# Four stages of a decoder kernel on one core: slot mixture, two attentions of sixteen heads of 64, and a gated attention

## The reference

```python
# L0 ffn (l0f): 64 experts x 32 slots = 2048 slots
logits = xn @ phi_w.T + phi_b            # (tokens, 2048), xn = layernorm(x)
dispatch = softmax over the 32 slots of each expert, per token
xt = dispatch^T @ xn  ->  experts  ->  val (2048, 128)
combine = softmax over the 64 experts at each slot number, per token
x += combine @ val
# L1 xattn (l1x) and L3 attn (l3a): 16 heads of 64
q, k, v = three projections of 128 -> 1024 (biases in l1x, keys of l1x from ctx)
x += softmax(causal(q k^T * scale)) v @ wf + bf
# L3 xattn (l3x): 8 heads of 16, gates from cumulative sums
D[i,j] = exp(-max(M_i - g_j, 0)) for j <= i, else 0
C = (q k^T) * D;  x += groupnorm(C v / max(|sum C|, ...))
```

## Time and profile before

| | us |
|---|---|
| median of 3 runs | 5007.74 (5003.48 to 5016.55) |
| profiled execution, its own time | 4999.0 |
| its span, first to last instruction | 4997.1 |
| window of the dispatch with its loads (574 to 936) | 362 |
| window of the combine (957 to 1410) | 453 |
| window of l1x (1661 to 2236) | 575 |
| window of l3a (3480 to 4032) | 552 |
| window of l3x, second part (4104 to 4318) | 214 |
| busy: PE 3581.9 (72%), DVE 3131.3 (63%), ACT 2404.7 (48%), POOL 2159.8 (43%) | |

### The profile page before, as it was taken

The page is one execution under the profiler, slowest core; times in us unless marked ns, Lnnn a source line. Parts: engine busy times, 40 slices in busy tenths (PEclk is TensorE's granted clock), DMA queues, the critical chain, the costliest instruction groups (busy, mean ns, idle before and its releaser), DMA issues. The chain is left out here.

```text
span 4997.1 us, 90315 instructions
## 1 busy us (share of the span) xinstructions
PE 3581.9 (72%) x28501; PEld 2648.4 (53%) x28501; DVE 3131.3 (63%) x5955; ACT 2404.7 (48%) x9569; POOL 2159.8 (43%) x2543
## 2 busy tenths in 40 slices
PE   7969677676679799971989223763999947369356
PEld 5646344465568577761656212563777723146356
DVE  6847588699957455557978622333666649878412
ACT  6959422344324477760469200221677722169235
POOL 3544288567634222221745054353232216545253
PEclk8979899888889899995989656886999969779578
DMA  6024100100000000000000510465000013120057
GB/s 82 2 38 57 31 1 1 42 1 1 1 11 2 21 4 4 4 2 3 3 13 10 92 40 29 138 191 163 1 0 0 0 43 105 44 42 2 13 196 253
DMA packets 365314, 210.42 MB, mean 42 GB/s; under 512 B 216339, under 2 KB 337452, under 8 KB 363668
## 3 DMA queue, kind: packets, MB, share of 16 engines
q1 hardware_dynamic: 351396, 180.67, 14.4%
q0 software_dynamic: 13568, 25.41, 1.5%
HBM read 156.40 MB, written 54.30 MB: 42 GB/s over the span
## 5 line engine op out<-in xcount | busy, mean ns | idle before, releaser
L2024 POOL TENSOR_TENSOR l1x_Sx<-l1x_Sx,l1x_sm 128x512 f32<-128x512 f32 x128 | 133.5, 1043 | 376.4 <-DVE l1x_sm L2167 376.4
L2024 POOL TENSOR_TENSOR l3a_Sx<-l3a_Sx,l3a_sm 128x512 f32<-128x512 f32 x128 | 133.5, 1043 | 353.5 <-DVE l3a_sm L2167 353.5
L2948 POOL DMA_INDIRECT l2f_results<-l2f_b_ys,l2f_b_xb x160 | 155.3, 971 | 217.3 <-DVE l2f_b_ys L2936 167.8
L1297 POOL TENSOR_TENSOR l0f_c_Z<-l0f_c_Z,l0f_c_shiftT 128x1024 f32<-128x1024 f32 x64 | 178.5, 2818 | 157.9 <-ACT l0f_c_shiftT L1219 157.9
L1175 PE MATMUL l0f_c_Y<-l0f_val,l0f_c_Z 128*128 128x128 f32 x1024 | 156.3, 325 | 113.7 <-DVE l0f_c_Z L1271 113.7
L1175 PEld LDWEIGHTS l0f_c_Y<-l0f_val,l0f_c_Z 128*128 128x128 f32 x1024 | 152.1, 240 | 120.2 <-DVE l0f_c_Z L1271 120.2
L2226 ACT ACTIVATE l3a_Sx<-l3a_Sx,l3a_nmx 128x128 f32<-128x128 f32 x512 | 199.2, 393 | 17.6 <-DVE l3a_nmx L2161 17.4
L2226 ACT ACTIVATE l1x_Sx<-l1x_Sx,l1x_nmx 128x128 f32<-128x128 f32 x512 | 200.1, 401 | 14.5 <-DVE l1x_nmx L2161 14.5
L1028 PE MATMUL l0f_acc<-l0f_d_xk,l0f_d_Z 128*128 128x128 f32 x1024 | 144.9, 285 | 82.9 <-POOL l0f_d_Z L995 82.6
L1028 PEld LDWEIGHTS l0f_acc<-l0f_d_xk,l0f_d_Z 128*128 128x128 f32 x1024 | 124.1, 191 | 149.5 <-POOL l0f_d_Z L995 148.8
L1098 ACT ACTIVATE l0f_d_Z<-l0f_d_Z 128x512 f32<-128x512 f32 x128 | 80.6, 630 | 242.2 <-POOL l0f_d_Z L990 242.2
(11 more groups left out here) (712 smaller groups left out, 12361.3 us busy)
## 6 DMA issues: line engine op xcount, KB each, us to landing
l3f_b_W<-in_l3f_we SPq DMA_DIRECT2D x72, 514.0 KB
l2f_b_W<-in_l2f_w SPq DMA_DIRECT2D x160, 192.0 KB
l3x_Mb<-l3x_dram_max SPq DMA_DIRECT2D x32, 512.0 KB, 3.4
l2f_sorted<-l2f_blank SPq DMA_DIRECT2D x1, 10400.0 KB, 58.6
l2f_b_xb<-l2f_sorted SPq DMA_DIRECT2D x40, 260.0 KB
...
```

The source lines that it names most:

```text
L1297: pool.tensor_tensor(piece(g, i), piece(g, i), bcast_mid(shiftT[:, g % 2, :], 4), ALU.subtract).then_inc(sub_done, 1)
L2024: pool.tensor_tensor(quad(Sx, s, q), quad(Sx, s, q), bcast_in(sm[:, s, 4 * q:4 * q + 4], P), ALU.mult).then_inc(w_done, 1)
L2948: pool.indirect_dma_start(Ys[:, :], bass.IndirectOffsetOnAxis(slot(j)[:, P:P + 1].bitcast(I32), 0), ys[:, j % 4, :], None, bounds_check=NB ...
```

## The change

*Dispatch and combine.* The 128 features of a normalised token add up to zero, so the last one is minus the sum of the others. `fold_bias` subtracts the last row of `phiT` from all rows and puts the slot bias in its place; row 127 of `XT` is constant 1 and only 127 rows of a transpose are copied into it. The matmul then gives logits with their bias. In the dispatch, ScalarE copies quarters 1 to 3 out of three banks; quarter 0 stays in PSUM, where DVE takes its maximum and subtracts it. In the combine, the maximum runs pair by pair, one operand in PSUM; all sums but the last step move to GpSimd, whose last addition becomes a second accumulated matmul with `quad`; the inverse stays in PSUM, and the normalisation reads it there.

*Attentions.* `Kexp` and its zeros go. The scores of a head are a matmul on its own 64 rows, into bank `S[r]` by strip r; heads are taken in two groups of eight. The query bias of l1x moves to DVE (one instruction for four chunks), the output bias to GpSimd, which adds it to x. A short matmul at the start of l1x spreads that bias.

*Gated attention.* GpSimd adds 1e30 to `Mb` where j > i, and ScalarE computes exp(-(Mb - g)) head by head with the gate as its bias; `gt` holds it so already. DVE keeps only the product with the scores. Mask comes before spread on GpSimd. The lower limit at zero is dropped, since M is a running maximum.

The core of the diff:

```diff
@@ dispatch_slots @@
-        L = [ps("L0"), ps("L1")]
+        banks = [ps("L0"), ps("L1"), ps("L2")]
+        L = [banks[0], banks[1], banks[2], banks[1]]
...
+                def first_quarter(b):
+                    wait(dve, l_mm, 4 * b + 1)
+                    nc.vector.tensor_reduce(mx[:, b % 2, 0, :], by_expert(L[0][:, :]), AXX, ALU.max).then_inc(first_max, 1)
+                    wait(dve, first_max, b + 1)
+                    wait(dve, tail_mm, 4 * b - 7)
+                    nc.vector.tensor_tensor(by_expert(quarter(b, 0)), by_expert(L[0][:, :]),
+                                            bcast_in(mx[:, b % 2, 0, :], PER), ALU.subtract).then_inc(first_sub, 1)
...
+                def evict(b, q):
+                    wait(act, tail_mm, 4 * b - 7 + q)
+                    wait(act, l_mm, 4 * b + q + 1)
+                    nc.scalar.copy(quarter(b, q), L[q][:, :]).then_inc(ev_done, 1)
...
@@ fold_bias @@
+            sp.dma_start(phiX[:, :], d["l0f_phiT"]).then_inc(phi_in, 16)
+            sp.dma_start(last[:, :], d["l0f_phiT"][P - 1:P].to_broadcast([P, SLOTS])).then_inc(phi_in, 16)
+            sp.wait_ge(minus_done, 1)
+            sp.dma_start(phiX[P - 1:P, :], d["l0f_phi_b"].rearrange("(a n) -> a n", a=1)).then_inc(row_in, 16)
...
+            pool.memset(XT[:, :], 1.0)
...
+            nc.vector.tensor_tensor(phiX[:, :], phiX[:, :], last[:, :], ALU.subtract).then_inc(minus_done, 1)
@@ combine_slots @@
+                def quad(g):
+                    wait(pe, sum_done, g + 1)
+                    wait(pe, w_done, 4 * g)
+                    for c in range(2):
+                        mm = nc.tensor.matmul(QS[:, 0:TOK], C.quad, add2[:, c, :], start=(c == 0), stop=(c == 1))
...
+                def pair_max(g, q):
+                    wait(dve, ev_done, 8 * g + q + 1)
+                    wait(dve, pair_done, 7 * g + q - 1)
+                    nc.vector.tensor_tensor(top[:, :, :], bank(g, q), pair(g, 0) if q == 1 else top[:, :, :],
+                                            ALU.max).then_inc(pair_done, 1)
...
+                    nc.vector.tensor_tensor(piece(g, i), piece(g, i), bcast_mid(QS[:, 0:TOK], 4),
                                             ALU.mult).then_inc(w_done, 1)
...
+                def sums(g):
+                    for i in range(2):
+                        wait(pool, exp_done, 4 * g + 2 * i + 2)
+                        pool.tensor_tensor(add8[:, 4 * i:4 * i + 4, :], piece(g, 2 * i), piece(g, 2 * i + 1),
+                                           ALU.add).then_inc(sum_steps, 1)
+                    wait(pool, sum_steps, 3 * g + 2)
+                    pool.tensor_tensor(add4[:, :, :], add8[:, 0:4, :], add8[:, 4:8, :], ALU.add).then_inc(sum_steps, 1)
+                    wait(pool, sum_steps, 3 * g + 3)
+                    wait(pool, qs_mm, g)
+                    pool.tensor_tensor(add2[:, :, :], add4[:, 0:2, :], add4[:, 2:4, :], ALU.add).then_inc(sum_done, 1)
@@ wide_head_attention @@
+                def scores(b, s, o):
+                    wait(pe, add_done, count(b, 4, 2 * o))
+                    for i in range(4):
+                        for r in range(2):
+                            rows = slice(64 * r, 64 * r + 64)
+                            mm = nc.tensor.matmul(S[r][:, i * P:(i + 1) * P], qT[rows, s, 4 * o + i, :],
+                                                  kT[rows, s, 4 * o + i, :], start=True, stop=True)
...
-                pool.memset(Kexp[:, :, :, :, :], 0.0).then_inc(zeros_done, 1)
...
@@ stage_l3_xattn @@
                     def mask(b, s):
-                        wait(pool, exp_done, count(b, 1, 1))
-                        pool.tensor_tensor(W[:, s, :, :], W[:, s, :, :], bcast_mid(C.tri, HEADS),
-                                           ALU.mult).then_inc(mask_done, 1)
+                        wait(pool, loaded[s], count_own(b, 32, 32))
+                        pool.tensor_tensor(Mb[:, s, :, :], Mb[:, s, :, :], bcast_mid(C.late, HEADS),
+                                           ALU.add).then_inc(mask_done, 1)
...
-                            ins = nc.vector.tensor_scalar(W[:, s, h, :], Mb[:, s, h, :], g, 0.0, ALU.subtract, ALU.max)
...
+                            ins = nc.scalar.activation(W[:, s, h, :], Mb[:, s, h, :], ACT.Exp, bias=g, scale=-1.0)
```

More of the change, by code:

```diff
@@ L998, in step, with subtract @@
-                def step(b, s, tail, head, front):
-                    for q in range(4):
-                        if front and ahead(b) and q == 1:
-                            ln.rstd(pool, shift(b, 2), s, C)
-                        if tail:
-                            normalise(shift(b, -1), 1 - s, q)
-                        if head:
-                            subtract(b, s, q)
+                def subtract(b, q):
+                    wait(pool, max_done, 3 * b + q)
+                    part = by_expert(quarter(b, q))
+                    pool.tensor_tensor(part, part, bcast_in(mx[:, b % 2, q, :], PER), ALU.subtract).then_inc(sub_done, 1)
@@ L1046, in _ @@
                                      skip_group_check=True)
-                normed_T(0, 0)
-                steps(step)
+                normed_T(0)
+                for i in range(-2, 4 * (NB + 1)):
+                    b, q = i // 4, i % 4
+                    if q == 0 and 0 <= b < NB - 1:
+                        normed_T(b + 1)
+                    if i + 2 < 4 * NB:
+                        logits((i + 2) // 4, (i + 2) % 4)
+                    if b > 0:
+                        dispatch(b - 1, q)
@@ L1307, in _ @@
                         subtract(g, i)
-                    for i in range(2):
-                        sum_first(g, i)
+                    sums(g)
         sems.clear()
@@ L2025, in normalise, with bias @@
                                        ALU.mult).then_inc(w_done, 1)
+                def bias(b):
+                    wait(pool, ln.done, count(b, 1, 1))
+                    pool.tensor_tensor(tile_of(X, b), tile_of(X, b), out_bias, ALU.add).then_inc(biased, 1)
                 def step(b, s, tail, head, front):
@@ L2056, in project_k, with project, project_q @@
-                def project_k(b, s):
+                def project(b, s, n, w, src, mm_done):
+                    for c in range(4 * n, 4 * n + 4):
+                        mm = nc.tensor.matmul(A[n][:, (c % 4) * P:(c % 4 + 1) * P], w[:, c * P:(c + 1) * P],
+                                              src[:, s, :], start=True, stop=True)
+                    mm.then_inc(mm_done, 1)
+                def project_q(b, s, n):
+                    wait(pe, xnt_done, count(b, 1, 1))
+                    wait(pe, v_done, count(b, 2, n - 1))
+                    project(b, s, n, wq, xnT, q_mm)
@@ new lines, in mask, with less_max @@
+                def mask(b, s, o):
+                    wait(dve, tp_mm, count(b, 4, 2 * o - 6))
+                    wait(dve, s_mm, count(b, 2, o + 1))
+                    for r in range(2):
+                        nc.vector.tensor_tensor(Sx[:, s, strip(o, r), :], heads(S[r][:, :]), bcast_mid(C.causal, 4),
+                                                ALU.add).then_inc(add_done, 1)
+                def less_max(b, s, o, r):
+                    wait(dve, add_done, count(b, 4, 2 * o + r + 1))
+                    nc.vector.tensor_reduce(nmx[:, s, strip(o, r)], Sx[:, s, strip(o, r), :], AXX, ALU.max, None, None,
@@ L2290, in _ @@
                 mm.then_inc(b_mm, 1)
+                pe.wait_ge(b_done, 1)
+                nc.tensor.matmul(pb[:, DM:2 * DM], C.ones[0:1, :], bf[0:1, :], start=True, stop=True).then_inc(wide_mm, 1)
             @block.vector
```

648 lines of the change are left out of this document (311 added, 337 removed).

## The result

The changed kernel took 4664.2 us (median of 4 runs, 4657.21 to 4670.01) against 5005.6 of the kernel before (5002.85 to 5016.55): ratio 0.9314, 95% interval 0.9294 to 0.9333. The forecast was 4660. The profiled execution spans 4662.9 us (before 4997.1), granted clock 0.859 (before 0.860).

A forecast was written before the change was run, and what follows sets the result against it. Five serial stages, each bound by its fullest engine or hand-over loop, were to gain 52 + 118 + 70 + 49 + 55 = 344 us: 4999.0 to 4655, forecast 4660 for the median, range 4600 to 4715.

The forecast's parts named there:

- Strips: l1x and l3a: score passes on paired 64-row strips start 0.055 us apart, 3.5 to 1.8 us a block.
- PSUM operands: Dispatch and combine: one operand in PSUM frees DVE from GpSimd; the combine's normalisation goes from 3.1 to 1.3 us.
- Combine: Combine stage: a group goes from 26.1 to 19.0 us, net gain 118 us.
- The wait of L1273: Combine: the one step with both operands in SBUF waits out a GpSimd instruction, 1.9 us a group.
- TensorE stays slow: Rival, combine: clock stays at 0.82, group 22 us, +45 us, total 4705; chance 0.06.
- Dispatch: Dispatch stage: a block goes from 10.44 to 8.6 us; net gain 52 us after the loads' loss.
- The loop that set the forecast: Dispatch: quarter 3's subtraction and exponential, next block's quarter 1 eviction and maximum, GpSimd instructions; 8.3 us with hand-overs.
- The loads' start: Before the dispatch: a subtraction of 2 us and a DMA landing of 2.5 us, 4.5 us lost.
- Attentions: l1x and l3a: blocks of 16.6 and 15.9 us both go to 14.4, net gains 70 and 49 us.
- the added waits of 0.2 a block: l1x and l3a: waits from the order of masks, maxima and key copies raise 14.2 to 14.4 us.
- Gated attention: l3x stage: a block goes from 6.17 to 4.4 us, gain 55 us.
- The loop: l3x: mask, spread and scores 5.9 us, then context load 2.5; with issue 8.8 us for two blocks.

The follow-up runs named there:

- the run with the clock mended: Changed kernel plus six small 128-column TensorE matmuls a combine group, ahead of the waits around the row maxima: combine stage 331.8 us against 335.8.

## Why the prediction was right

*What is shown and what is read off.* Two edits were taken back by themselves: the order of strips (75 us) and the place of the inverse (44.5 us), 120 of the 338 us. That the rest comes from the work taken off DVE, TensorE and GpSimd is read off the rows and not shown by a run; no run puts the bias addition of the dispatch or DVE's part of the exponent in l3x back.

*Strips.* Right, with its price: 1.16 us for 16 passes, and undoing the order alone gives 75 us back. What it takes is that neighbours in the order use different strips; the narrower matmuls alone do not give it.

*PSUM operands.* Right: 1.212 us forecast as 1.3, and with the operand back in SBUF the stage is 44.5 us longer. In the dispatch the subtraction of quarter 0 took 0.692 us, forecast 0.66.

*Combine.* Mechanism right, the total off by 6 us because two terms were mis-sized. The wait of L1273 was 1.16 us a group, not 1.9: it asks at another point of GpSimd's rhythm in each group (0.42 to 2.45 us). Since the group has 19.4, some 1.1 us came in its place that the sum did not have. TensorE at the lower level for 38 of 291 us is at most 0.3 of it, by the run with the clock mended; the rest I can't tell apart. The rival "TensorE stays slow" (22 us a group) did not come true: the clock went from 0.82 to 0.93, and mending half of what was left gave at most 4 us, not 45. What keeps the group at 19.4 is that TensorE's chain and GpSimd's 17.8 us are within 1.6 us of each other.

*Dispatch.* 6 us better. The loop that set the forecast (8.3 to 8.6) goes through the eviction of quarter 1, and moving that eviction did nothing. Measured: DVE has 0.907 x 8.47 = 7.7 us busy (90.68 of 100 us from 700 to 800, forecast 7.3; L258 has 1.107 us, its counterpart before had 0.598) and waits 0.47 for quarter 3, while GpSimd (91.56 of 100) waits 0.7 for DVE's reciprocals. Moving quarter 3's eviction gave 18 us, by the way the two engines then met and not by the wait that it was to remove. So the period of 8.47 came out near the forecast by luck. The loads' start cost 4.9 against 4.5.

*Attentions.* 70.9 and 46.7 against 70 and 49; the added waits of 0.2 a block were too careful in l1x, and the execution at hand had 7 us more at the end of l3a, and 5 more in l1x, with the clock at 0.5 there.

*Gated attention.* 5 us short of the forecast. The loop was right in form, but the mask on `Mb` takes 2.364 us where I took the 2.00 of the product with `W`, and the load of the maxima, which I left out, closes the same loop at 4.5 us a block. The trace before had that load, 3.4 us from issue to landing in the median.
